# A state-space scan kernel on Trainium2: token order for `u`, exponentials written in the scan's buffer, and the state reduction moved ahead of VectorE's pieces

## The chip, the cores and the metric

One core of one Trainium2 chip. The metric is the time of one execution on the device in microseconds (us), lower is better. The program is one launch that holds four stages of a small network. The change touches only the first, the state-space stage, which runs from the start to about 4,100 us of 6,212.

## The reference, cut to what matters

The first stage is a Mamba block over x of shape (2, 4096, 512), with 1024 inner channels, 16 states per channel and a 4-tap convolution along time:

```python
hidden, gate = jnp.split(proj, 2, axis=-1)          # proj = layernorm(x) @ in_proj_w
h = causal 4-tap depthwise conv(hidden) + conv_b
hs = silu(h)
dt, Bm, Cm = split(hs @ x_proj_w)                   # each then rms-normalised
dt = softplus(dt @ dt_proj_w + dt_proj_b)
dA = exp(dt[..., None] * A)                         # (batch, time, 1024, 16)
dBu = (dt * u)[..., None] * Bm                      # u = hs
s_t = dA_t * s_{t-1} + dBu_t                        # the scan over time
y_t = sum_n s_t[n] * C_t[n]
out = ((y + u * D) * silu(gate)) @ out_proj_w
```

Everything is float32. Three more stages follow (a sum of eight matrix products, a chunked linear attention, a spline layer). They are the same in both kernels.

## The kernel before, in words

**Tiling.** Time is cut into chunks of T = 512 tokens, 8 per batch and 16 in all. One chunk is one *period*; the two batches take turns, and the middle periods are a hardware loop. The 1024 channels lie as G = 8 groups of 128 partitions. A *unit* k = 0..31 is one channel group with four of its 16 states; eight units belong to a pair of channel groups. A unit is a tile `s[k % 4]` of 128 partitions by 4 states by 512 tokens, so four units are in flight at most.

**One unit.**
- TensorE (PE) forms `BU`, the product of dt·u and B, with 16 small matmuls into four PSUM banks (`b_product`, L747). There is one `BU`, so it starts only when all scans of the unit before have read it (`scan_done`).
- ScalarE (ACT) computes the four exponentials (L507) into `DA`, two buffers of 512 tokens. Exponential n + 2 therefore waits for scan n.
- VectorE (DVE) runs the four scans (L661), `s = DA * s_before + BU`, each started from `state`.
- VectorE copies the last token of the four scans into `state` with a small reduction (L666), which raises `state_saved`. The copy is needed because the next step overwrites `s`.
- GpSimd (POOL) waits for `state_saved`, then multiplies `s` in place by the broadcast `Cb`, in two instructions of 128x1024 (L339, `z_ready`).
- TensorE adds the products of two units into `Y` by matmuls with an identity (`y_sum`, L765), in two parts, `sums(k)`, that stand behind `b_product(k)` or behind the other work of unit k. They raise `sum_done`. A slot of `s` is free when its sums are through: before, the scans waited for that.

**Work between the units.** Everything else of this period and of the next is cut into pieces and given to unit numbers by hand-written tables (`GATE_AT`, `HID_AT`, `DT_AT`, `Y_AT` and so on). Each engine walks its units in order and does its piece at its place. On VectorE `piece(k)` stands behind the scans of unit k and *ahead of* the state reduction of unit k. Its pieces are:
- k = 14..21, `conv` of one channel group: a copy of 3 elements (L543), another of 3 (L547, after a wait for ScalarE's `hid`), three `scalar_tensor_tensor` over 512 tokens (L551) with a drain between them;
- k = 0, 12, 19, 29: `dt_floor` (L581); k = 3, 13, 22, 30: `dt_max` (L586); k = 4, 13, 22, 30: `dt_times_u` (L591);
- k = 2, 10: statistics of the layer norm (L525 to L530), and k = 4, 11: its application, two `tensor_scalar` (L535);
- k = 26, 27: sums and scaling of the x projection (L557 to L573); k = 1, 9, 17, 25: `y_out` (L609), which reads PSUM; k = 3, 6, 10, 11: the residual (L599), which reads PSUM.

GpSimd has small work of its own, at k = 2 and 10 (`ln_power`, L304) and k = 26 (`ssm_power`, L308), ahead of the multiplication of that unit, and at k = 28, 29, 30 and 0 behind it (`spread_b`, L314).

On ScalarE the pieces `late(k - 1)` and `early(k)` stood between the exponentials of unit k, and `long_piece(k - 1)`, which may hold a silu over 128x2048 between two loads of the activation table, behind them.

**Two orders of the tokens.** `u` was kept block by block: token q·4 + b of a chunk at place b·128 + q. The x projection and the transposes of dt·u want blocks of 128 columns, one of each fourth token, and read them contiguously. The convolution, the product with dt and ScalarE's first write of `u` (L385) work in token order, so they step through `u` by 128 elements.

Of the kernel before, what the change touches and what calls it, by code (L numbers as in the profile page):

```python
# [58 lines left out]
def mamba_block(nc, x, in_w, chan, xproj_w, dt_w, out_w, eye, tokmask, x1):  # L59
# [21 lines left out]
    with ctx:  # L81
# [27 lines left out]
        spread = sb("spread", [P, NQ, TB, 32, 4])  # L109

        s = [sb(f"s{i}", [P, 4, T]) for i in range(SLOTS)]
        DA = [sb(f"DA{i}", [P, T]) for i in range(2)]
# [76 lines left out]
        def in_time(ap):  # L189
            return ap.rearrange("p (b q) -> p q b", b=TB)  # L190

        def by_block(ap):
            return ap.rearrange("p (q b) -> p b q", b=TB)
# [158 lines left out]
        def _(act):  # L352
# [26 lines left out]
            def take_hid(ring_, m, period, c_next, slot):  # L379

                wait(act, conv_done, c_next * G + m - 1)

                act.wait_ge(ring_.full, ring_.filled(("hid", m), period))
                bank = PJ[ring_.bank(("hid", m))]
                nc.scalar.activation(in_time(u[slot][:, m, :]), bank[:].rearrange("p (q b) -> p q b", b=TB), ACT.Identity,  # L385
                                     bias=ch[:, m, 4:5], scale=ch[:, m, 3:4])
                nc.scalar.copy(hid[m % 2][:, 3:T + 3], bank[:]).then_inc(ring_.taken["act"], 1)

            def take_gate(ring_, m, period):
# [57 lines left out]
            def body(i, b, c, first, last):  # L447
# [51 lines left out]

                for k in range(U):  # L500
                    p, nq, gi = k // UP, k % UP // 2, k % 2
                    for n in range(4):
                        if k % UP == 0 and n == 0:
                            wait(act, dt_ready, PAIRS * c + p + 1)

                        wait(act, scan_done, 4 * (c * U + k) + n - 1)
                        nc.scalar.activation(DA[n % 2][:], dt[p % 2][:, gi, :], ACT.Exp,  # L507
                                             scale=ch[:, 2 * p + gi, 7 + 4 * nq + n:8 + 4 * nq + n]).then_inc(da_ready, 1)
                        if n == 1 and k > 0:
                            late(k - 1)  # L510
                        if n == 1 and k == 0 and not first:
                            wait(act, y_ready, (c - 1) * G + 6)
                            take_gate(steady, 5, c - 1)
                        if n == 2:
                            early(k)
                    long_piece(k - 1)

            periods(act, body)

        @block.vector  # L520
        def _(dve):
# [16 lines left out]

            def conv(ring_, m, period, b_next, slot):

                out = in_time(u[slot][:, m, :])
                h_ = hid[m % 2]
                nc.vector.tensor_copy(h_[:, 0:3], hist[:, b_next, m, :])  # L543
                s_, v = ring_.emptied(("hid", m), period)
                dve.drain()
                dve.wait_ge(s_, v)
                nc.vector.tensor_copy(hist[:, b_next, m, :], h_[:, T:T + 3])  # L547
                for tap in range(3):
                    if tap > 0:
                        dve.drain()  # L550
                    last_ = nc.vector.scalar_tensor_tensor(out, h_[:, tap:tap + T].rearrange("p (q b) -> p q b", b=TB),  # L551
                                                           ch[:, m, tap:tap + 1], out, ALU.mult, ALU.add)
                last_.then_inc(conv_done, 1)

            def ssm_sums(c_next):
# [32 lines left out]
            def dt_times_u(p, n, c_of, slot):  # L588
                dve.wait_ge(u_ready, 2 * (c_of + 1))
                dve.wait_ge(dt_ready, n + 1)  # L590
                nc.vector.tensor_tensor(dts[:].rearrange("p g (b q) -> p g b q", b=TB),  # L591
                                        dt[p % 2][:].rearrange("p g (q b) -> p g b q", b=TB),
                                        u[slot][:, 2 * p:2 * p + 2, :].rearrange("p g (b q) -> p g b q", b=TB), ALU.mult
                                        ).then_inc(dtu_ready, 1)

            def add_res(ring_, j, period, c_prev):
# [27 lines left out]
            def body(i, b, c, first, last):  # L624
# [50 lines left out]
        def _(pe):  # L675
# [21 lines left out]
            def x_proj(ring_, tb, period, c_next, slot):  # L697
                use = ("xp", tb // 2)
                if tb % 2 == 0:
                    wait(pe, u_ready, 2 * (c_next + 1))  # L700
                    bank_of(ring_, use, period)
                bank = PJ[ring_.bank(use)]
                for g in range(G):
                    last_ = nc.tensor.matmul(bank[:, tb % 2 * SP_:(tb % 2 + 1) * SP_], u[slot][:, g, tb * P:(tb + 1) * P],  # L704
                                             w_xp[:, g, :], start=(g == 0), stop=(g == G - 1))
                if tb % 2 == 1:
                    last_.then_inc(ring_.full, 1)
# [20 lines left out]
            def turn_dtu(ring_, p, n, period):  # L728
                wait(pe, dtu_ready, n + 1)
                for gi in range(2):  # L730
                    bank = bank_of(ring_, (f"tr{p}", gi), period)
                    for tb in range(TB):
                        last_ = nc.tensor.transpose(bank[:, tb * P:(tb + 1) * P], dts[:, gi, tb * P:(tb + 1) * P], ident[:])
                    last_.then_inc(ring_.full, 1)

            def out_proj(bank, j, part, slot):
# [15 lines left out]
            def skip_product(p, slot):  # L752
                for r in range(2):
                    rows = slice(64 * r, 64 * r + 64)
                    for gi in range(2):
                        nc.tensor.matmul(by_block(Y[r][y_rows(r, gi), :]), skip_w[rows, 2 * p + gi, :],
                                         u[slot][rows, 2 * p + gi, :].rearrange("p (b q) -> p b q", b=TB),
                                         start=True, stop=False, tile_position=(64 * r, y_rows(r, gi).start))

            def y_sum(k_even, part):  # L760
# [1050 lines left out]
```

## Time and profile before

| what | us |
|---|---|
| median of 3 runs | 6220.06 (6214.05 to 6225.43) |
| the profiled execution | 6213.6 |
| its span from first to last instruction | 6211.7 |
| busy: PE, DVE, ACT, POOL | 5083.5, 5140.9, 2792.8, 3227.9 |
| scans (DVE, L661), 2048 of them | 2470.6 |
| z products (POOL, L339), 1024 of them | 2390.9 |

Busy is the sum of the times in which an engine has an instruction running. "L661" is line 661 of the kernel before. In a timeline a row is a run of like instructions: start, duration of the whole run, engine, line, operation, output<-inputs, count, and in brackets the idle time before it with what ended it.

### The profile page before, as it was taken

What the parts mean: (1) busy time and instruction counts of PE and PEld (TensorE: products, weight loads), DVE (VectorE), ACT (ScalarE), POOL (GpSimd) and SP (SyncE); (2) the same over time, 40 slices, a digit from 0 to 9 for tenths busy, and PEclk for the clock granted to TensorE, in tenths of its full rate; (3) what the DMA queues carried; (4) which work ended last, traced back from release to release, by engine and by line L of the source; (5) the groups of instructions that cost most, each with busy time, mean ns of one, the idle gap of its engine ahead of it and who ended that gap; (6) DMA issues with size and microseconds to landing.
All of it is one profiled execution on the core that took longest, in us unless ns stands there. A gap on an engine that the chain in (4) does not pass through costs nothing. (4 is left out here: it accounts for less than half of the span.)

```text
span 6211.7 us, 111888 instructions
## 1 busy us (share of the span) xinstructions
PE 5083.5 (82%) x41157; PEld 2990.7 (48%) x41157; DVE 5140.9 (83%) x7468; ACT 2792.8 (45%) x4180; POOL 3227.9 (52%) x1675
## 2 busy tenths in 40 slices
PE   6788988888888888888888888748888888888832
PEld 3344444444444444434434444317777776777722
DVE  4888888888888888888888888757888888888888
ACT  3656555556565555565555555512222222222200
POOL 1566665665666656657566566623333333333322
PEclk9999999999999999999999999869999999899955
DMA  2121221222212222222122221230000000000024
GB/s 81 71 96 62 89 93 65 95 73 79 89 69 89 81 77 89 76 80 89 71 89 81 77 89 72 86 130 19 23 23 21 21 23 23 19 23 23 18 96 142
DMA packets 139965, 421.36 MB, mean 68 GB/s; under 512 B 38368, under 2 KB 39904, under 8 KB 106592
## 3 DMA queue, kind: packets, MB, share of 16 engines
q1 hardware_dynamic: 136672, 411.75, 18.9%
q8 instruction: 268, 4.39, 0.3%
q10 hardware_dynamic: 2816, 3.51, 0.2%
q14 instruction: 209, 1.71, 0.1%
HBM read 361.99 MB, written 53.22 MB: 67 GB/s over the span
## 5 line engine op out<-in xcount | busy, mean ns | idle before, releaser
L339 POOL TENSOR_TENSOR s<-s,Cb 128x1024 f32<-128x1024 f32 x1024 | 2390.9, 2356 | 1362.8 <-DVE state L666 1353.3
L661 DVE TENSOR_TENSOR_SCAN s<-DA,state,BU 128x512 f32<-128x512 f32 x2048 | 2470.6, 1263 | 497.6 <-PE BU L747 301.7
L507 ACT ACTIVATE DA<-dt,ch 128x512 f32<-128x512 f32 x2048 | 1453.5, 720 | 1570.1 <-DVE s L661 1566.6
L765 PE MATMUL Y<-s,ident 64*64 64x512 f32 x8192 | 1013.0, 610 | 124.7 <-POOL s L339 124.0
L693 PE MATMUL PJ<-xnT,w_in 128*128 128x512 f32 x2048 | 998.9, 634 | 44.2 <-ACT dtuT L371 42.5
L747 PE MATMUL BU<-spread,dtuT 32*128 32x128 f32 x16384 | 624.0, 290 | 287.8 <-DVE s L661 285.5
L747 PEld LDWEIGHTS BU<-spread,dtuT 32*128 32x128 f32 x16384 | 524.0, 193 | 677.6 <-DVE s L661 544.1
L693 PEld LDWEIGHTS PJ<-xnT,w_in 128*128 128x128 f32 x2048 | 388.8, 199 | 549.0 <-issue 453.1
L765 PEld LDWEIGHTS Y<-s,ident 64*64 64x64 f32 x8192 | 280.0, 134 | 620.6 <-issue 584.9
L738 PE MATMUL PJ<-w_out,u 128*128 128x512 f32 x1024 | 481.3, 615 | 1.8 <-DVE u L609 1.5
L551 DVE SCALAR_TENSOR_TENSOR u<-hid,ch,u 128x512 f32<-128x512 f32 x384 | 434.5, 1132 | 19.1
L1121 POOL TENSOR_TENSOR x1t<-x1t,bias_b 128x512 f32<-128x512 f32 x64 | 81.0, 1266 | 525.7 <-DVE xa L1293 525.7
L1474 PE MATMUL bank<-w_high_o,aTs 128*128 128x512 f32 x512 | 212.2, 481 | 129.4 <-DVEq L1396 129.4
L738 PEld LDWEIGHTS PJ<-w_out,u 128*128 128x128 f32 x1024 | 188.7, 194 | 242.1 <-issue 231.1
L1115 POOL TENSOR_TENSOR r_t<-x,x3n 128x512 f32<-128x512 f32 x64 | 82.5, 1290 | 344.7 <-DVE x3n L1293 344.7
L1236 ACT ACTIVATE junk<-bank 128x512 f32<-128x512 f32 x64 | 38.3, 598 | 380.2 <-PE bank L1546 380.2
L1474 PEld LDWEIGHTS bank<-w_high_o,aTs 128*128 128x128 f32 x512 | 119.5, 233 | 167.3 <-issue 139.0
L1474 PE MATMUL bank<-w_high_f,xaT 128*128 128x512 f32 x512 | 195.8, 445 | 2.6 <-DVE xaT L1298 2.6
L385 ACT ACTIVATE u<-PJ,ch 128x512 f32<-128x512 f32 x128 | 162.1, 1266 | 54.7 <-PE PJ L693 52.6
L704 PE MATMUL PJ<-w_xp,u 128*128 128x160 f32 x1024 | 165.7, 322 | 22.4 <-ACT dtuT L371 12.6
L1172 ACT COPY qk_all<-bank 128x512 f32<-128x512 f32 x128 | 75.3, 588 | 224.0 <-PE bank L1474 224.0
L704 PEld LDWEIGHTS PJ<-w_xp,u 128*128 128x128 f32 x1024 | 154.4, 205 | 40.7 <-issue 26.4
(218 smaller groups left out, 7667.2 us busy)
## 6 DMA issues: line engine op xcount, KB each, us to landing
Cb<-bc SPq DMA_DIRECT2D x256, 1024.0 KB, 4.8
res<-in_x SPq DMA_DIRECT2D x64, 256.0 KB, 4.8
x<-res SPq DMA_DIRECT2D x64, 256.0 KB, 5.3
x1t<-x SPq DMA_DIRECT2D x64, 256.0 KB, 2.6
out<-r_t SPq DMA_DIRECT2D x64, 256.0 KB, 2.0
xt<-in_x SPq DMA_DIRECT2D x31, 512.0 KB, 5.3
x_all<-out SPq DMA_DIRECT2D x16, 512.0 KB, 4.1
scm<-out SPq DMA_DIRECT2D x16, 512.0 KB, 4.7
```

What stands on the lines that cost most here:

```text
L339: nc.gpsimd.tensor_tensor(pair, pair, Cb[q % 2][:, 2 * part * T:2 * part * T + 2 * T], ALU.mult).then_inc(z_ready, 1)
L385: nc.scalar.activation(in_time(u[slot][:, m, :]), bank[:].rearrange("p (q b) -> p q b", b=TB), ACT.Identity, bias=ch[:, m, 4:5], scale=ch[ ...
L507: nc.scalar.activation(DA[n % 2][:], dt[p % 2][:, gi, :], ACT.Exp, scale=ch[:, 2 * p + gi, 7 + 4 * nq + n:8 + 4 * nq + n]).then_inc(da_rea ...
L551: last_ = nc.vector.scalar_tensor_tensor(out, h_[:, tap:tap + T].rearrange("p (q b) -> p q b", b=TB), ch[:, m, tap:tap + 1], out, ALU.mult ...
L661: nc.vector.tensor_tensor_scan(s[k % SLOTS][:, n, :], DA[n % 2][:], BU[:, n::4], state[:, b, k, n:n + 1], ALU.mult, ALU.add).then_inc(scan ...
L693: last_ = nc.tensor.matmul(bank[:], w_in[:, kb, lo:lo + P], xnT[:, kb, :], start=(kb == 0), stop=(kb == KB - 1))
L704: last_ = nc.tensor.matmul(bank[:, tb % 2 * SP_:(tb % 2 + 1) * SP_], u[slot][:, g, tb * P:(tb + 1) * P], w_xp[:, g, :], start=(g == 0), st ...
L738: last_ = nc.tensor.matmul(bank[:], u[slot][:, g, j * P:(j + 1) * P], w_out[:, g, :], start=(g == 0), stop=(g == G - 1))
L747: last_ = nc.tensor.matmul(BU[:, i * T:(i + 1) * T].rearrange("p (t b n) -> p b t n", b=TB, n=4)[:, tb], dtuT[rows, gi, tb, :], spread[row ...
L765: last_ = nc.tensor.matmul(Y[r][y_rows(r, gi), :], ident[rows, rows], s[(k_even + gi) % SLOTS][rows, n, :], start=False, stop=(n == 3 and ...
L1115: nc.gpsimd.tensor_tensor(r_t[s_][:], x3[s_][:], x3n[s_][:], ALU.add).then_inc(S["r_ready"], 1)
L1474: last_ = nc.tensor.matmul(b_[:], src[part][:, k, :], wt, start=(k == 0 and i == 0), stop=(k == KB - 1 and i == 2))
```

## The change

Four edits, all in the state-space stage.

1. `u` is in token order everywhere. ScalarE, the convolution and the product with dt step by 1; the x projection's weights and the transposes' inputs are now read with a step of 4 elements (`by_block`), and the skip product reads and writes straight.
2. ScalarE writes the exponentials into the scan's own buffer `s[k % 4]`; the scan works in place and `DA` is gone. The wait for a free slot (`sum_done`) moves from VectorE's scans to ScalarE's exponentials, and their wait for `scan_done` is gone.
3. ScalarE computes the four exponentials of unit k in one go. `long_piece(k - 1)`, `late(k - 1)` and `early(k)` follow, in this order.
4. On VectorE the state reduction comes straight behind the scans of its unit, and `piece(k)` behind the reduction.

```diff
@@ ScalarE, take_hid
-                nc.scalar.activation(in_time(u[slot][:, m, :]), bank[:].rearrange("p (q b) -> p q b", b=TB), ACT.Identity,
-                                     bias=ch[:, m, 4:5], scale=ch[:, m, 3:4])
+                nc.scalar.activation(u[slot][:, m, :], bank[:], ACT.Identity, bias=ch[:, m, 4:5], scale=ch[:, m, 3:4])
...
@@ ScalarE, body
                 for k in range(U):
                     p, nq, gi = k // UP, k % UP // 2, k % 2
+                    if k % UP == 0:
+                        wait(act, dt_ready, PAIRS * c + p + 1)
+                    wait(act, sum_done, c * U + k // 2 * 2 - 2)
                     for n in range(4):
-                        if k % UP == 0 and n == 0:
-                            wait(act, dt_ready, PAIRS * c + p + 1)
-
-                        wait(act, scan_done, 4 * (c * U + k) + n - 1)
-                        nc.scalar.activation(DA[n % 2][:], dt[p % 2][:, gi, :], ACT.Exp,
+                        nc.scalar.activation(s[k % SLOTS][:, n, :], dt[p % 2][:, gi, :], ACT.Exp,
                                              scale=ch[:, 2 * p + gi, 7 + 4 * nq + n:8 + 4 * nq + n]).then_inc(da_ready, 1)
-                        if n == 1 and k > 0:
-                            late(k - 1)
...
-                        if n == 2:
-                            early(k)
                     long_piece(k - 1)
+                    if k > 0:
+                        late(k - 1)
...
+                    early(k)
@@ VectorE, conv
-                out = in_time(u[slot][:, m, :])
+                out = u[slot][:, m, :]
...
-                    last_ = nc.vector.scalar_tensor_tensor(out, h_[:, tap:tap + T].rearrange("p (q b) -> p q b", b=TB),
-                                                           ch[:, m, tap:tap + 1], out, ALU.mult, ALU.add)
+                    last_ = nc.vector.scalar_tensor_tensor(out, h_[:, tap:tap + T], ch[:, m, tap:tap + 1], out,
+                                                           ALU.mult, ALU.add)
@@ VectorE, dt_times_u
-                nc.vector.tensor_tensor(dts[:].rearrange("p g (b q) -> p g b q", b=TB),
-                                        dt[p % 2][:].rearrange("p g (q b) -> p g b q", b=TB),
-                                        u[slot][:, 2 * p:2 * p + 2, :].rearrange("p g (b q) -> p g b q", b=TB), ALU.mult
+                nc.vector.tensor_tensor(dts[:], dt[p % 2][:], u[slot][:, 2 * p:2 * p + 2, :], ALU.mult
@@ VectorE, body
                 for k in range(U):
-                    wait(dve, sum_done, c * U + k // 2 * 2 - 2)
                     wait(dve, dbu_ready, c * U + k + 1)
                     for n in range(4):
                         wait(dve, da_ready, 4 * (c * U + k) + n + 1)
-                        nc.vector.tensor_tensor_scan(s[k % SLOTS][:, n, :], DA[n % 2][:], BU[:, n::4],
+                        nc.vector.tensor_tensor_scan(s[k % SLOTS][:, n, :], s[k % SLOTS][:, n, :], BU[:, n::4],
                                                      state[:, b, k, n:n + 1], ALU.mult, ALU.add
                                                      ).then_inc(scan_done, 1)
-                    piece(k)
                     wait(dve, scan_done, 4 * (c * U + k + 1))
                     nc.vector.tensor_reduce(state[:, b, k, :], s[k % SLOTS][:, :, T - 1:T], AX.X, ALU.max
                                             ).then_inc(state_saved, 1)
+                    piece(k)
@@ TensorE: x_proj reads by_block(u[slot][:, g, :])[:, tb], turn_dtu by_block(dts[:, gi, :])[:, tb],
@@ skip_product writes Y and reads u straight.
```

**VectorE, a unit with a convolution.** Before, from the scans of the first such unit on:

```order
L661 SCALAR_TENSOR_TENSOR s<-DA,state,BU 128x512 [waits da_ready,dbu_ready,sum_done]
L661 SCALAR_TENSOR_TENSOR s<-DA,state,BU 128x512 [waits da_ready] x3
L543 COPY hid<-hist 128x3
L547 COPY hist<-hid 128x3 [waits proj_taken_act_steady]
L551 SCALAR_TENSOR_TENSOR u<-hid,ch,u 128x128x4 x3
L666 TENSOR_REDUCE state<-s 128x4 [waits scan_done]
```

And now, at the same place:

```order
L651 SCALAR_TENSOR_TENSOR s<-s,state,BU 128x512 [waits da_ready,dbu_ready]
L651 SCALAR_TENSOR_TENSOR s<-s,state,BU 128x512 [waits da_ready] x3
L655 TENSOR_REDUCE state<-s 128x4 [waits scan_done]
L536 COPY hid0<-hist 128x3
L540 COPY hist<-hid0 128x3 [waits proj_taken_act_steady]
L544 SCALAR_TENSOR_TENSOR u1<-hid0,ch,u1 128x512 x3
```

The rows with SCALAR_TENSOR_TENSOR on `s` are the scans. The reduction that frees GpSimd moved from behind the three passes over `u` to directly behind the scans, and the wait for `sum_done` is gone from the first scan.

**ScalarE, around the first silu of the gate (k = 5 and 6).** Before:

```order
L507 ACTIVATE DA0<-dt0,ch 128x512 [waits scan_done]
L507 ACTIVATE DA1<-dt0,ch 128x512 [waits scan_done]
L491 ACT_TABLE_LOAD
L491 ACTIVATE gate<-gate 128x2048
L492 ACT_TABLE_LOAD
L507 ACTIVATE DA0<-dt0,ch 128x512 [waits scan_done]
```

And now:

```order
L501 ACTIVATE s2<-dt0,ch 128x512 [waits sum_done]
L501 ACTIVATE s2<-dt0,ch 128x512 x3
L486 ACT_TABLE_LOAD
L486 ACTIVATE gate<-gate 128x2048
L487 ACT_TABLE_LOAD
L501 ACTIVATE s3<-dt0,ch 128x512 [waits sum_done]
L501 ACTIVATE s3<-dt0,ch 128x512 x3
```

Each exponential waited for a scan; now a unit's four wait once, for the sums that free their slot.

## Rows read from the trace of the kernel before

**Rows 1.** Stretch, us; busy us (count) PE, PEld, DVE, ACT, POOL; PE clock; DMA

```profile
400.00:3700.00 3300.00, 2892.06 (x25117) 1379.67 (x25109) 2841.09 (x3241) 1950.24 (x2632) 2079.57 (x941) 0.98 0.23 82
```

**Rows 2.** Who waited for whom, 400 to 3700 us: total us, times, longest

```profile
DVE s L661 <- PE BU L747: 240.6, 181, 3.8
DVE s L661 <- ACT DA L507: 134.7, 124, 3.3
```

**Rows 3.** Timeline of DVE: unit 14 of the ninth period, and unit 22's start

```profile
2216.57 4.78 DVE L661 TENSOR_TENSOR_SCAN s<-DA,state,BU 128x512 f32<-128x512 f32 x4
2221.27 0.15 DVE L543 COPY hid<-hist 128x3 f32<-128x3 f32 x1
2221.57 0.17 DVE L547 COPY hist<-hid 128x3 f32<-128x3 f32 x1 [0.15 <-issue]
2221.65 3.63 DVE L551 SCALAR_TENSOR_TENSOR u<-hid,ch,u 128x512 f32<-128x512 f32 x3
2225.20 0.15 DVE L666 TENSOR_REDUCE state<-s 128x4 f32<-128x4 f32 x1
...
2288.57 4.78 DVE L661 TENSOR_TENSOR_SCAN s<-DA,state,BU 128x512 f32<-128x512 f32 x4
```

**Rows 4.** Timeline of POOL, the product of the same unit 14

```profile
2225.43 4.67 POOL L339 TENSOR_TENSOR s<-s,Cb 128x1024 f32<-128x1024 f32 x2 [4.03 <-DVE state L666]
```

**Rows 5.** Timelines of POOL and DVE near 889 us

```profile
885.82 4.67 POOL L339 TENSOR_TENSOR s<-s,Cb 128x1024 f32<-128x1024 f32 x2 [1.99 <-DMA Cb<-bc]
889.60 1.97 DVE L586 TENSOR_TENSOR dt<-dt,dts 128x1024 f32<-128x1024 f32 x1 [0.24 <-DVE res L599]
```

**Rows 6.** Timelines of DVE and POOL near 5894 us, in a later stage

```profile
5893.54 0.69 DVE L1408 TENSOR_TENSOR rc<-qk_all,rot 128x512 f32<-128x512 f32 x1
5893.70 1.68 POOL L1126 TENSOR_TENSOR xf<-xf,gamma_b 128x512 f32<-128x512 f32 x1 [7.31 <-DVE xf L1293]
5894.14 1.52 DVE L1410 TENSOR_TENSOR rs<-qk_all,rot 128x256 f32<-128x256 f32 x1
```

**Rows 7.** Timelines of POOL and DVE near 4228 us, in a later stage

```profile
4227.67 1.05 POOL L1138 TENSOR_TENSOR kd<-qk_all,k_dec 128x512 f32<-128x512 f32 x1
4227.97 1.03 DVE L1293 TENSOR_SCALAR xb<-x_all,mv_b,rd_b 128x512 f32<-128x512 f32 x1
4228.68 1.46 POOL L1147 TENSOR_TENSOR kvd<-kv,kv_dec 128x512 f32<-128x512 f32 x1
```

**Rows 8.** Groups by line and shape, 1000 to 3800 us: busy us, mean ns, idle before

```profile
L551 DVE SCALAR_TENSOR_TENSOR u<-hid,ch,u 128x512 f32<-128x512 f32 x278 | 314.8, 1132 | 13.9
L704 PEld LDWEIGHTS PJ<-w_xp,u 128*128 128x128 f32 x729 | 111.1, 207 | 23.1 <-ACT dtuT L371 11.5 <-issue 10.1
L591 DVE TENSOR_TENSOR dts<-dt,u 128x1024 f32<-128x1024 f32 x45 | 92.1, 2046 | 3.5
L586 DVE TENSOR_TENSOR dt<-dt,dts 128x1024 f32<-128x1024 f32 x45 | 55.1, 1223 | 13.9 <-ACT dts L423 11.4 <-DVE res L599 2.5
```

**Rows 9.** Timeline of DVE, scan starts of units 3, 4, 5, 11, 12, 13, 27, 28

```profile
2134.18 4.79 DVE L661 TENSOR_TENSOR_SCAN s<-DA,state,BU 128x512 f32<-128x512 f32 x4 [0.82 <-PE BU L747]
...
2141.00 4.78 DVE L661 TENSOR_TENSOR_SCAN s<-DA,state,BU 128x512 f32<-128x512 f32 x4
...
2148.62 4.78 DVE L661 TENSOR_TENSOR_SCAN s<-DA,state,BU 128x512 f32<-128x512 f32 x4
...
2194.43 4.79 DVE L661 TENSOR_TENSOR_SCAN s<-DA,state,BU 128x512 f32<-128x512 f32 x4
...
2201.16 3.62 DVE L661 TENSOR_TENSOR_SCAN s<-DA,state,BU 128x512 f32<-128x512 f32 x3
...
2207.90 4.79 DVE L661 TENSOR_TENSOR_SCAN s<-DA,state,BU 128x512 f32<-128x512 f32 x4 [0.98 <-PE BU L747]
...
2324.55 4.79 DVE L661 TENSOR_TENSOR_SCAN s<-DA,state,BU 128x512 f32<-128x512 f32 x4 [1.22 <-PE BU L747]
...
2331.16 3.62 DVE L661 TENSOR_TENSOR_SCAN s<-DA,state,BU 128x512 f32<-128x512 f32 x3 [0.30 <-PE BU L747]
```

More of the change, by code:

```diff
@@ L111, in mamba_block @@
         s = [sb(f"s{i}", [P, 4, T]) for i in range(SLOTS)]
-        DA = [sb(f"DA{i}", [P, T]) for i in range(2)]
         Cb = [sb(f"Cb{i}", [P, 4 * T]) for i in range(2)]
@@ L187, in y_rows @@
             return slice(at, at + 64)
-        def in_time(ap):
-            return ap.rearrange("p (b q) -> p q b", b=TB)
         def by_block(ap):
@@ L501, in body @@
                     p, nq, gi = k // UP, k % UP // 2, k % 2
+                    if k % UP == 0:
+                        wait(act, dt_ready, PAIRS * c + p + 1)
+                    wait(act, sum_done, c * U + k // 2 * 2 - 2)
                     for n in range(4):
-                        if k % UP == 0 and n == 0:
-                            wait(act, dt_ready, PAIRS * c + p + 1)
-                        wait(act, scan_done, 4 * (c * U + k) + n - 1)
-                        nc.scalar.activation(DA[n % 2][:], dt[p % 2][:, gi, :], ACT.Exp,
+                        nc.scalar.activation(s[k % SLOTS][:, n, :], dt[p % 2][:, gi, :], ACT.Exp,
                                              scale=ch[:, 2 * p + gi, 7 + 4 * nq + n:8 + 4 * nq + n]).then_inc(da_ready, 1)
-                        if n == 1 and k > 0:
-                            late(k - 1)
-                        if n == 1 and k == 0 and not first:
-                            wait(act, y_ready, (c - 1) * G + 6)
-                            take_gate(steady, 5, c - 1)
-                        if n == 2:
-                            early(k)
-                    long_piece(k - 1)
+                    long_piece(k - 1)
+                    if k > 0:
+                        late(k - 1)
+                    elif not first:
+                        wait(act, y_ready, (c - 1) * G + 6)
+                        take_gate(steady, 5, c - 1)
+                    early(k)
             periods(act, body)
@@ L703, in x_proj @@
                 for g in range(G):
-                    last_ = nc.tensor.matmul(bank[:, tb % 2 * SP_:(tb % 2 + 1) * SP_], u[slot][:, g, tb * P:(tb + 1) * P],
+                    last_ = nc.tensor.matmul(bank[:, tb % 2 * SP_:(tb % 2 + 1) * SP_], by_block(u[slot][:, g, :])[:, tb],
                                              w_xp[:, g, :], start=(g == 0), stop=(g == G - 1))
@@ L732, in turn_dtu @@
                     for tb in range(TB):
-                        last_ = nc.tensor.transpose(bank[:, tb * P:(tb + 1) * P], dts[:, gi, tb * P:(tb + 1) * P], ident[:])
+                        last_ = nc.tensor.transpose(bank[:, tb * P:(tb + 1) * P], by_block(dts[:, gi, :])[:, tb], ident[:])
                     last_.then_inc(ring_.full, 1)
@@ L755, in skip_product @@
                     for gi in range(2):
-                        nc.tensor.matmul(by_block(Y[r][y_rows(r, gi), :]), skip_w[rows, 2 * p + gi, :],
-                                         u[slot][rows, 2 * p + gi, :].rearrange("p (b q) -> p b q", b=TB),
+                        nc.tensor.matmul(Y[r][y_rows(r, gi), :], skip_w[rows, 2 * p + gi, :], u[slot][rows, 2 * p + gi, :],
                                          start=True, stop=False, tile_position=(64 * r, y_rows(r, gi).start))
```

## The prediction

> **What bounds the kernel now.** I read the busy time by stretch first. From 400 to 3700 us, inside the state-space stage, VectorE is busy 2841 of 3300 us and TensorE 2892, the matmul figure being a modelled one, at a granted clock of 0.98 of full speed [rows 1]. No engine is free to spare, so order matters. Then the waits: VectorE waits 240.6 us there for `BU` and 134.7 us for exponentials [rows 2]. A period lasts about 249 us (45 products with dt in 2800 us, four per period [rows 8]), so the stretch holds 13.2 periods, and these waits are 18.2 and 10.2 us of each. The `BU` wait is structural: one `BU`, made only after the unit's last scan. The change leaves it. The wait for exponentials is what edits 2 and 3 can remove.
>
> The third view is the timeline of one unit with a convolution, 14 [rows 3, 4]. Scans start at 2216.57; the first copy starts at 2221.27, so 4.70 us later VectorE turns to its piece; three passes over `u` take 3.63; only then comes the reduction, at 2225.20, and the product on GpSimd starts 0.23 later and runs 4.67 for its two halves. It fits under the next unit's 4.78 of scans. So in the kernel before, VectorE's pieces run while GpSimd stands still, and GpSimd runs beside scans. Eight such units take 2288.57 − 2216.57 = 72.0 us [rows 3].
>
> **Two engines that exclude each other.** Three places tell what happens when a piece does meet GpSimd. At 889.60 `dt_max`, two inputs in SBUF, starts while the product runs until 885.82 + 4.67 = 890.49. It ends at 891.57, 1.08 later [rows 5]; its mean is 1.223 [rows 8]. It did nothing until GpSimd was through, then needed its own time less 0.14. At 5894.14 a product of 256 elements starts beside a GpSimd instruction that ends at 5895.38 and is itself done at 5895.66: 1.52 us, of which 1.24 are waiting [rows 6]. There GpSimd had asked at 5893.70, under the VectorE instruction L1408 that ended at 5894.23; VectorE's next instruction was ready at once, and GpSimd still came first. At 4228 it is the reverse: GpSimd's L1138 ends at 4228.72, its next one, L1147, is already there at 4228.68, and VectorE's, waiting since 4227.97, ends first, at 4229.00 [rows 7]. So whoever waits gets the next turn, and they alternate by whole instructions. The Trainium skill ("SBUF — State Buffer", Who interferes with whom) says that a VectorE instruction with two SBUF inputs or in a two-port mode, and a GpSimd one, block each other fully, the first to start going first. It gives no order among those who wait; by its words alone both this forecast and rival A stand, and rows 6 and 7 choose between them.
>
> Scans read one input from SBUF and one from PSUM, and rows 3 and 4 have them beside the product at full speed. `y_out` and the residual read PSUM too, and count as free.
>
> **The change part by part** (times from the start of the reduction in its new place, 4.70 us after the unit's first scan).
>
> *Convolution units, 14 to 21.* The first copy starts at 0.08 and ends at 0.23. GpSimd starts at 0.23 [rows 4]. The second copy would start at 0.38 (0.30 after the first [rows 3]): I take it that it waits, until 0.23 + 2.34 = 2.57. GpSimd's second half is queued by then and goes next, to 4.95. First pass: in token order it costs 0.69, the price of a contiguous two-input operation of 512 elements (L1408 [rows 6]), less 0.14, so it ends at 5.50. Two passes more, 0.69 + 0.05 each: 6.98. The next scan starts 0.08 before the end of what stands ahead of it (the reduction starts 0.08 before the passes' end [rows 3]). Unit: 4.70 + 6.98 − 0.08 = 11.6 us. Eight of them and 0.6 for `dt_floor` in unit 19: 93.4, against 72.0: **+21.4 us**. Without the lock the passes would have saved 3 x (1.13 − 0.69) = 1.3 per unit.
>
> *Other units with pieces that need both ports* [rows 9]:
> - Unit 3: residual, then `dt_max`, behind one half of the product: 2.57 + 1.09 = 3.66; unit 8.3 against 6.82: +1.5.
> - Unit 4: `ln_apply` gets in first (0.08 to 0.61), a half to 2.95, second `ln_apply` 3.23, the other half 5.57, `dt_times_u` 1.09 more, 6.66. Unit 11.3 against 7.62: +3.7. The product with dt itself falls from 2046 to about 1223 ns [rows 8].
> - Unit 11: `ln_apply` twice around one half, 3.23, residual 0.67: 8.5 against 6.73: +1.8.
> - Unit 13: `dt_max` first, to 1.30, a half to 3.64, `dt_times_u` to 4.73: 9.35 against 8.67: +0.7. Units 22 and 30 hold the same two pieces: +0.8 each.
> - Unit 27: three scalings. The product of unit 26 is still running (it stands behind `ssm_power`) until about 0.9; the first scaling ends at 1.4, then half, scaling, half, scaling: 6.2. Unit 10.8 against 6.61: +4.2.
> - `dt_floor` at 0, 12 and 29 starts 0.15 before GpSimd can: nothing for VectorE.
>
> Together 13.5. **Lost per period: 34.9 us.**
>
> *Exponentials.* A unit's four no longer wait for scans. The gate is `sum_done`: unit k even needs the sums of the pair before last, which TensorE issues right behind the `BU` of unit k − 1, about a unit ahead. The silu over 2048 columns with its two table loads then falls on exponentials that are already there. Of the 10.2 us, 1 lies in the convolution units and is in their 72.0; some waits end in the `BU` wait instead. I take **7.8 us gained per period**, bounds 0 and 10.2. Late is then only `BU`. Nothing queues behind ScalarE's one new wait, since it can be a unit ahead.
>
> *ScalarE's write of `u`* gets cheaper and is hidden on an engine busy 59% [rows 1]: nothing. *Earlier products* cannot help where VectorE sets the pace: nothing. No DMA changes; `Cb` loads are released by the products and have a unit to spare.
>
> *TensorE's reads with a step of 4.* 32 weight loads of 207 ns per period [rows 8] and 32 transposes. No row of before shows such a read. Bounds: nothing, or as much as the step of 128 costs VectorE, a factor of 2046/1223 = 1.7: 32 x 0.14 = 4.5 us for the loads, and about the same for the transposes. I take nothing, since nearly all units then go at VectorE's pace, with TensorE waiting for scans; the upper end would be +9 x 15 = 135 us if none were hidden. The Trainium skill ("SBUF — State Buffer", SBUF: two separate sides) has lines of 16 bytes and a penalty for each access that crosses to a new one; a step of 4 floats does so every time, and by that the sum would move towards this upper end.
>
> *Prologue.* 8 groups of 3 passes, 0.44 less each [rows 6, 8], 10.6 in all, a part of it under the projections: −8.
>
> **Sum.** Net per period 34.9 − 7.8 = +27.1. Fifteen periods prepare a next chunk: +406. The last has units 3, 4, 13 and 22 without norm and convolution: about −5. With the prologue: 6213.6 + 406 − 5 − 8 = 6606.6 for the profiled execution, which lies 6.5 under the median of the runs; I predict **6610 us**, some 6% slower.
>
> **Own range of this case.** The passes may stay at 1.13 (+1.3 per unit, +160), TensorE's reads +135, exponentials 0 to 10.2 gained (+117 or −36), a second copy that does not wait (first pass ahead of the second half, −0.3 per unit, −36), two scalings going together in unit 27 and at `ln_apply` (−2.3 each, −70). Not all come at once: 6450 to 6780.
>
> **Rivals.**
> - **A, faster: VectorE keeps its turn.** If GpSimd cannot get in between two instructions of one piece, a convolution unit pays one half only: 2.6 + 3 x 0.74 − 0.14 gives 9.3, +0.4 each over 72.0/8 = 9.0, +3 in all; unit 3 +1.5; units 4, 11, 13, 22, 27 and 30 about −3 together. With −7.8: −6.3 per period, −95, less 8: 6115 by the median. Decides: whether the passes run in a row after the first half. For it: the pauses between them are only 0.05. Against: rows 6. 7%.
> - **B, faster: no conflict to speak of.** Passes of 0.74 beside GpSimd: convolution units about 7.8 by TensorE's own work, −10; the other pieces −3; −7.8. Times 15: about −310, 5900. Rows 5 to 7 speak against it. 5%.
> - **C, much slower: the turns cost more than their halves**, or the exponentials, tied to sums that wait for slower products, become late. Each 1 us more in eight units is +120: 6800 to 7000. 5%.
> - **D, the pieces have moved where GpSimd is mostly waiting anyway**, for `Cb` or an earlier product, and both effects about cancel: 6200 to 6450. A wait of 1.99 for `Cb` is there [rows 5], but the one of unit 14 is for the reduction [rows 4]. 6%.
>
> **How the numbers follow.** The forecast has 77%. Range for 8 in 10: its own, widened a little at the lower end for D: 6420 to 6790. A measurement of this kernel tells 0.2% from no change. Faster: A, B and little of D, 0.13. Same: 0.02. Slower: 0.85.
>
> **What would show it.** In the changed profile the passes over `u` must have a mean near (5.50 − 0.46 + 2 x 0.74)/3, some 2.2 us, though they are cheaper; the product on GpSimd must start 0.2 behind each unit's scans; its waits for `state` must be gone from the top, and VectorE's waits for exponentials be near nothing; units 14 to 21 must take 11 to 12 us each and unit 5, with no piece, as long as before. Passes of 0.7 us beside a running product would prove the lock wrong, and a mean of 1.3 with 9.3 us units rival A.

## The result and the profile after

The changed kernel takes 6723.91 us (median of 4 runs, 6717.08 to 6729.63) against 6222.25 before, a ratio of 1.081, 95% interval 1.079 to 1.083. It is slower, as forecast, and 114 us above the predicted 6610. Its profiled execution has a span of 6715.3 us.

The groups of instructions by line and shape, 1000 to 3800 us of the changed kernel (busy us, mean ns of one | idle before), answer to [rows 8]:

```profile
L544 DVE SCALAR_TENSOR_TENSOR u<-hid,ch,u 128x512 f32<-128x512 f32 x240 | 331.7, 1382 | 11.9
L540 DVE COPY hist<-hid 128x3 f32<-128x3 f32 x80 | 175.9, 2199 | 13.8 <-issue 10.1
L584 DVE TENSOR_TENSOR dts<-dt,u 128x1024 f32<-128x1024 f32 x40 | 129.5, 3238 | 3.1
L579 DVE TENSOR_TENSOR dt<-dt,dts 128x1024 f32<-128x1024 f32 x39 | 58.2, 1493 | 2.1 <-DVE res L590 2.1
L528 DVE TENSOR_SCALAR xt<-xt,mv,rstd 128x512 f32<-128x512 f32 x38 | 57.7, 1560 | 0.0
L566 DVE TENSOR_TENSOR xt<-xt 128x64 f32<-128x64 f32 x20 | 46.6, 2366 | 0.0
L694 PEld LDWEIGHTS PJ<-w_xp,u 128*128 128x128 f32 x640 | 151.6, 329 | 13.2 <-issue 8.1 <-ACT dtuT L367 3.8
```

A pass over `u` steps by 1 now and is yet longer, 1382 ns against 1132. The product with dt, whose access became contiguous too, went from 2046 to 3238. The clearest row is L540: a copy of three elements takes 2.2 us on average. None of these computes longer: with GpSimd out of the way (first experiment below) the same four groups take 749, 169, 1223 and 530 ns (L544, L540, L584, L528). They stand on VectorE, issued, and wait for GpSimd. The last row is TensorE's and another matter: the weight loads with a step of 4 cost 329 ns, not 207.

One unit shows how. The timeline of VectorE in the changed kernel, unit 15 of a period (as [rows 3]):

```profile
2504.48 4.79 DVE L651 TENSOR_TENSOR_SCAN s<-s,state,BU 128x512 f32<-128x512 f32 x4
2509.30 0.16 DVE L655 TENSOR_REDUCE state<-s 128x4 f32<-128x4 f32 x1
2509.37 0.16 DVE L536 COPY hid<-hist 128x3 f32<-128x3 f32 x1
2509.68 2.23 DVE L540 COPY hist<-hid 128x3 f32<-128x3 f32 x1 [0.15 <-issue]
2511.82 4.56 DVE L544 SCALAR_TENSOR_TENSOR u<-hid,ch,u 128x512 f32<-128x512 f32 x3
2516.30 4.79 DVE L651 TENSOR_TENSOR_SCAN s<-s,state,BU 128x512 f32<-128x512 f32 x4
```

and that of GpSimd beside it (as [rows 4]):

```profile
2509.53 4.66 POOL L335 TENSOR_TENSOR s<-s,Cb 128x1024 f32<-128x1024 f32 x2 [7.17 <-DVE state L655]
```

The product starts 0.23 after the reduction. The second copy, issued at 2509.68, ends at 2511.91, when the first half is through; the second half goes next, to 2514.19, and the passes only end at 2516.38. The unit takes 11.82 us against the 9.0 of before.

Who waited for whom, 400 to 3700 us of the changed kernel, answers to [rows 2]:

```profile
DVE s L651 <- PE BU L737: 264.2, 180, 5.7
DVE s L651 <- ACT s L501: 16.2, 7, 3.2
```

The waits for exponentials are down from 134.7 us to 16.2: edits 2 and 3 do what they say. GpSimd's own waits for `state`, the same view before and after, did not shrink:

```profile
POOL s L339 <- DVE state L666: 1101.0, 385, 5.6
POOL s L335 <- DVE state L655: 1231.4, 295, 7.8
```

Scan starts in the changed kernel, from the timeline of VectorE (as [rows 9]; units 3, 4, 5, 11, 12, 13, 14, 22, 23, 24, 25, 27, 28 of one period):

```profile
2689.63 4.79 DVE L651 TENSOR_TENSOR_SCAN s<-s,state,BU 128x512 f32<-128x512 f32 x4 [0.68 <-PE BU L737]
...
2698.56 4.78 DVE L651 TENSOR_TENSOR_SCAN s<-s,state,BU 128x512 f32<-128x512 f32 x4
...
2709.70 4.78 DVE L651 TENSOR_TENSOR_SCAN s<-s,state,BU 128x512 f32<-128x512 f32 x4
...
2753.33 4.80 DVE L651 TENSOR_TENSOR_SCAN s<-s,state,BU 128x512 f32<-128x512 f32 x4 [0.32 <-DVE res L590]
...
2762.20 4.79 DVE L651 TENSOR_TENSOR_SCAN s<-s,state,BU 128x512 f32<-128x512 f32 x4 [0.32 <-DVE res L590]
...
2768.37 4.79 DVE L651 TENSOR_TENSOR_SCAN s<-s,state,BU 128x512 f32<-128x512 f32 x4 [0.55 <-PE BU L737]
...
2777.75 4.78 DVE L651 TENSOR_TENSOR_SCAN s<-s,state,BU 128x512 f32<-128x512 f32 x4
...
2873.16 4.79 DVE L651 TENSOR_TENSOR_SCAN s<-s,state,BU 128x512 f32<-128x512 f32 x4
...
2882.53 4.78 DVE L651 TENSOR_TENSOR_SCAN s<-s,state,BU 128x512 f32<-128x512 f32 x4
...
2889.44 4.79 DVE L651 TENSOR_TENSOR_SCAN s<-s,state,BU 128x512 f32<-128x512 f32 x4 [1.94 <-PE BU L737]
...
2900.11 4.79 DVE L651 TENSOR_TENSOR_SCAN s<-s,state,BU 128x512 f32<-128x512 f32 x4 [5.69 <-PE BU L737]
...
2914.52 4.79 DVE L651 TENSOR_TENSOR_SCAN s<-s,state,BU 128x512 f32<-128x512 f32 x4 [1.33 <-PE BU L737]
...
2925.24 4.78 DVE L651 TENSOR_TENSOR_SCAN s<-s,state,BU 128x512 f32<-128x512 f32 x4
```

The eight convolution units take 2873.16 − 2777.75 = 95.4 us. Unit 24 takes 2900.11 − 2889.44 = 10.67, of which VectorE waits 5.69 for `BU`.

### The profile page after: what moved, and what is told of

Same layout as the page of the kernel before. It is cut to its first block and busy times, and to the rows that moved or that the text cites. A ratio compares the mean times of both kernels' runs of the same rounds, so it can differ in the third digit from the quotient of the medians.

```text
span 6715.3 us, 110904 instructions
## 1 busy us (share of the span) xinstructions
PE 5323.7 (79%) x41157; PEld 3151.7 (47%) x41157; DVE 5720.9 (85%) x7468; ACT 2611.6 (39%) x4180; POOL 3377.3 (50%) x1675
## 5 line engine op out<-in xcount | busy, mean ns | idle before, releaser
L335 POOL TENSOR_TENSOR s<-s,Cb 128x1024 f32<-128x1024 f32 x1024 | 2539.7, 2502 | 1678.4 <-DVE state L655 1670.1
L651 DVE TENSOR_TENSOR_SCAN s<-s,state,BU 128x512 f32<-128x512 f32 x2048 | 2452.7, 1259 | 426.3 <-PE BU L737 382.4
L501 ACT ACTIVATE s<-dt,ch 128x512 f32<-128x512 f32 x2048 | 1305.3, 712 | 921.6 <-PE Y L754 920.4
L754 PE MATMUL Y<-s,ident 64*64 64x512 f32 x8192 | 1088.6, 650 | 17.9 <-POOL s L335 17.6
L544 DVE SCALAR_TENSOR_TENSOR u<-hid,ch,u 128x512 f32<-128x512 f32 x384 | 532.3, 1386 | 19.1
L540 DVE COPY hist<-hid 128x3 f32<-128x3 f32 x128 | 248.5, 1942 | 34.2 <-ACT hid L382 15.8
L694 PE MATMUL PJ<-w_xp,u 128*128 128x160 f32 x1024 | 252.9, 404 | 9.6 <-issue 6.5
L694 PEld LDWEIGHTS PJ<-w_xp,u 128*128 128x128 f32 x1024 | 243.0, 329 | 27.2 <-issue 20.8
L367 ACT COPY dtuT<-PJ 128x512 f32<-128x512 f32 x128 | 68.8, 588 | 394.0 <-PE PJ L723 394.0
L584 DVE TENSOR_TENSOR dts<-dt,u 128x1024 f32<-128x1024 f32 x64 | 203.1, 3174 | 5.0
```

The source lines that it names most:

```text
L335: nc.gpsimd.tensor_tensor(pair, pair, Cb[q % 2][:, 2 * part * T:2 * part * T + 2 * T], ALU.mult).then_inc(z_ready, 1)
L501: nc.scalar.activation(s[k % SLOTS][:, n, :], dt[p % 2][:, gi, :], ACT.Exp, scale=ch[:, 2 * p + gi, 7 + 4 * nq + n:8 + 4 * nq + n]).then_i ...
L584: nc.vector.tensor_tensor(dts[:], dt[p % 2][:], u[slot][:, 2 * p:2 * p + 2, :], ALU.mult).then_inc(dtu_ready, 1)
L651: nc.vector.tensor_tensor_scan(s[k % SLOTS][:, n, :], s[k % SLOTS][:, n, :], BU[:, n::4], state[:, b, k, n:n + 1], ALU.mult, ALU.add).then ...
L754: last_ = nc.tensor.matmul(Y[r][y_rows(r, gi), :], ident[rows, rows], s[(k_even + gi) % SLOTS][rows, n, :], start=False, stop=(n == 3 and ...
```

## The experiments

Each ratio is to the kernel before on the same chip. A unit's length is the time from its first scan to the next unit's, averaged over 12 middle periods of the trace.

**Undoing edit 4 alone.**

```diff
+                    piece(k)
                     wait(dve, scan_done, 4 * (c * U + k + 1))
                     nc.vector.tensor_reduce(state[:, b, k, :], s[k % SLOTS][:, :, T - 1:T], AX.X, ALU.max
                                             ).then_inc(state_saved, 1)
-                    piece(k)
```

> The changed kernel with edit 4 alone undone: piece(k) stands ahead of the state reduction again. Theory (VectorE's two-port pieces and GpSimd's product exclude each other): convolution units fall from 11.8 us to about 8.0, where TensorE's own work of 7 to 9 us sets them, units 3, 4, 11, 13, 22, 27 and 30 lose another 13 us, so some 44 us per period go: about 6070 us, 2 to 3% below the kernel before. Rival (scans in place, the new gate on the exponentials or TensorE's reads with a step of 4 are what costs): still above 6500 us.

Measured: 5924.77 us, ratio 0.954 (0.952 to 0.956). The rival is out: edits 1 to 3 together are good for 4.6%, and edit 4 turns that into a loss of 8%. It came 145 us lower than I expected: the convolution units are 7.5 us in most, 62 for the eight, and the units behind a long one are shorter too (more below). Its passes are free of waiting:

```profile
L544 DVE SCALAR_TENSOR_TENSOR u<-hid,ch,u 128x512 f32<-128x512 f32 x264 | 197.7, 749 | 13.1
```

This row of its groups by line and shape, 1000 to 3800 us, gives the own price of a pass, 749 ns. The 1382 of the changed kernel is this and 0.63 us of waiting.

**Edit 4 alone on the kernel before.**

```diff
-                    piece(k)
                     wait(dve, scan_done, 4 * (c * U + k + 1))
                     nc.vector.tensor_reduce(...).then_inc(state_saved, 1)
+                    piece(k)
```

> The kernel before with edit 4 alone. Theory: the passes over u still cost 1.13 us each, so a convolution unit is 4.70 + 4.95 + 0.99 + 2 x 1.18 - 0.08 = 12.9 us against 9.0, +32 per period; the other units with two-port pieces +15; about 45 us x 15, so 6900 us. Rival (edit 4 is harmless and edits 1 to 3 made the kernel slower): 6220 us.

Measured: 7034.94 us, ratio 1.133 (1.131 to 1.135). One moved instruction of 0.15 us costs 13%. The period went from 249.5 to 304.0 us, 54.5 more where the terms I had named are 32 and 15. The convolution units, 13.1 each, are the 32. The other units whose pieces meet GpSimd (3, 4, 11, 13, 22, 27, 30) are 20.9, not 15; units 13 and 30 alone add 3.8 and 3.7, since `dt_max` waits there as well (2531 ns on average, 1493 in the changed kernel). Units without a lock add a little, as 31 (9.8 against 7.9) and 5 (7.3 against 6.4). Its row for the passes, same view and stretch:

```profile
L551 DVE SCALAR_TENSOR_TENSOR u<-hid,ch,u 128x512 f32<-128x512 f32 x216 | 377.8, 1749 | 10.7
```

1749 is the 1132 of before and 0.62 us of waiting, the same surcharge as with the contiguous pass.

**The reduction early, GpSimd's start late.**

```diff
-                    nc.vector.tensor_reduce(state[:, b, k, :], s[k % SLOTS][:, :, T - 1:T], AX.X, ALU.max
-                                            ).then_inc(state_saved, 1)
+                    nc.vector.tensor_reduce(state[:, b, k, :], s[k % SLOTS][:, :, T - 1:T], AX.X, ALU.max)
                     piece(k)
+                    dve.drain().then_inc(state_saved, 1)
```

> The changed kernel; the reduction stays directly behind the scans, but the signal that lets GpSimd start is given by a drain behind piece(k). Theory (it is GpSimd's start that costs, not the place of the reduction): as e1_piece_first within 0.5%, about 6080 us. Rival (the reduction between scans and piece costs by itself, or the order of VectorE's instructions does): near 6720 us.

Measured: 5985.2 us, ratio 0.964 (0.962 to 0.965). VectorE's instructions have the order of the changed kernel, and the loss is gone: it is when GpSimd starts. It is 1.0% above the kernel with the piece first, twice what I had allowed. A convolution unit is 0.5 us longer. Some 0.2 of this is the reduction in its new place: the piece starts 4.91 us after the unit's first scan, not 4.70, so a small part of the rival is true. The other 0.3 is a wait of the next scan for nothing the profile names (44.8 us in 3300), which the kernel with the piece first has not; the drain is the only thing added there. The row is from who waited for whom, 400 to 3700 us, of this kernel (total us, times, longest):

```profile
DVE s L651 <- issue: 44.8, 156, 0.6
```

Per period it is 6.0 us above the kernel with the piece first (236.8 against 230.8), some 90 us over fifteen. The total differs by only 60, because everything behind the last scan, the same code in both, took 2105 us here and 2128 there. No run tells why.

**GpSimd's product in quarters.**

```diff
-                    for part in range(2):
-                        pair = s[k % SLOTS][:, 2 * part:2 * part + 2, :].rearrange("p n t -> p (n t)")
-                        nc.gpsimd.tensor_tensor(pair, pair, Cb[q % 2][:, 2 * part * T:2 * part * T + 2 * T],
-                                                ALU.mult).then_inc(z_ready, 1)
+                    for n in range(4):
+                        last_ = nc.gpsimd.tensor_tensor(s[k % SLOTS][:, n, :], s[k % SLOTS][:, n, :],
+                                                        Cb[q % 2][:, n * T:(n + 1) * T], ALU.mult)
+                        if n % 2 == 1:
+                            last_.then_inc(z_ready, 1)
```

> The changed kernel with GpSimd's product in four instructions of 512 elements, not two of 1024 (signals as before, at the second and the fourth). Theory (turns alternate by whole instructions): VectorE waits for one quarter, about 1.2 us, where it waited for a half, 2.3: units 4 and 27 lose 2.3 us each, 3, 11, 13, 22 and 30 1.15 each, the convolution units 0.4 each, some 13 us per period, about 6530 us. Rival (VectorE waits until the whole product is through): no change, 6720 us, or a little slower by GpSimd's fixed cost per instruction.

Measured: 6516.83 us, ratio 1.049 (1.047 to 1.051). The period fell from 284.1 to 271.1 us, by about the 13 I had named; unit 4 from 11.15 to 8.97, unit 27 from 10.72 to 8.85, unit 13 from 9.38 to 8.29, most convolution units from 11.84 to 11.38. A convolution unit in this kernel's timelines of VectorE and of GpSimd:

```profile
2401.33 1.15 DVE L541 COPY hist<-hid 128x3 f32<-128x3 f32 x1 [0.15 <-issue]
2402.39 5.17 DVE L545 SCALAR_TENSOR_TENSOR u<-hid,ch,u 128x512 f32<-128x512 f32 x3
...
2401.18 5.83 POOL L334 TENSOR_TENSOR s<-s,Cb 128x512 f32<-128x512 f32 x4 [5.53 <-DVE state L656]
```

The copy now waits 1.15 where it waited 2.23, and GpSimd's four quarters spread to 5.83 because VectorE's turns lie between them. Turns by whole instructions are shown; "VectorE waits until the product is through" is out.

**Edits 2 and 3 alone, and edit 1 alone,** both on the order of before (piece, then reduction). The first is the changed ScalarE body and the in-place scans on a block-ordered `u`; the second is all of the diff that concerns `u`, with `DA` kept.

```diff
@@ e5, against the kernel before
-                        nc.vector.tensor_tensor_scan(s[k % SLOTS][:, n, :], DA[n % 2][:], BU[:, n::4],
+                        nc.vector.tensor_tensor_scan(s[k % SLOTS][:, n, :], s[k % SLOTS][:, n, :], BU[:, n::4],
... and ScalarE's body as in the whole diff
@@ e6, against the kernel before
-                out = in_time(u[slot][:, m, :])
+                out = u[slot][:, m, :]
... and all other lines of the whole diff that read or write u
```

> The kernel before with edits 2 and 3 alone (exponentials in the scan's buffer, a unit's four in one go); u in block order, the piece ahead of the reduction. Theory: the waits for exponentials go (10.2 us per period in the profile before, 7.8 of them worth something, mostly units 6 and 9): 6210 - 7.5 x 15, about 6100 us. Rival (the waits turn into waits for BU and nothing is won): 6200 us.

Measured: 6023.04 us, ratio 0.970 (0.968 to 0.971), 77 below my figure. The period is 237.5 us, 12.0 less, more than the 10.2 of VectorE's own waits for exponentials: units 6 and 9 give 2.1 and 1.9, units 28 and 29 1.2 and 1.3, and unit 23, where before TensorE waited for ScalarE's copies, 1.0. From 1000 to 3800 us TensorE's waits for these copies fall from 8.9 us to under 1 ahead of the transposes of dt·u and from 9.8 to 2.9 ahead of the x projection. That ScalarE serves TensorE earlier because it is no longer tied to scans is my reading of this, not a separate test.

> The kernel before with edit 1 alone (u in token order). Theory: passes of 0.75 us take 1.2 us from each convolution unit, as far as TensorE's own work lets it (-9 per period), the product with dt -2, TensorE's reads with a step of 4 +4 (units 24 and 25, as in the changed kernel's trace): -7 x 15, about 6100 us. Rival (convolution units stay as they are, bound by TensorE or ScalarE): 6260 us.

Measured: 6146.31 us, ratio 0.989 (0.988 to 0.991). A gain of 1.0%, where I expected 1.8%. The convolution units gave the 9 us per period I had named (8.7), but units 24 and 25 are 3.1 and 0.8 us longer, as in the changed kernel, and unit 23 another 1.0.

**TensorE's reads contiguous.**

```diff
@@ x_proj, against e1_piece_first
-                    last_ = nc.tensor.matmul(bank[...], by_block(u[slot][:, g, :])[:, tb],
+                    last_ = nc.tensor.matmul(bank[...], u[slot][:, g, tb * P:(tb + 1) * P],
@@ turn_dtu
-                        last_ = nc.tensor.transpose(bank[...], by_block(dts[:, gi, :])[:, tb], ident[:])
+                        last_ = nc.tensor.transpose(bank[...], dts[:, gi, tb * P:(tb + 1) * P], ident[:])
```

The expectation names only the x projection. As built, the kernel reads the transposes' inputs contiguously too. The transposes stand in units 7, 15, 23 and 31; units 24 and 25 hold none, so what they show is the x projection's alone.

> e1_piece_first with one more change: the x projection reads its weights contiguously out of u (128 neighbouring places instead of each fourth), so it projects other tokens than the reference does. Theory (the step of 4 lengthens the weight loads from 205 to 329 ns and makes unit 24 3.2 us longer, unit 25 0.8): about 4 us per period less, 5865 us, and unit 24 back at 7.5 us. Rival (unit 24 is long for another reason, such as the order of TensorE's work or its clock): 5925 us.

Measured: 5837.4 us, ratio 0.940 (0.938 to 0.941), 87 us under the kernel with the step of 4 (that one ran on another chip; the kernel before takes 6209 us there and 6212 here). Unit 24 is back at 7.53, unit 25 at 6.18, unit 23 at 6.17. The groups of this kernel, 1000 to 3800 us:

```profile
L694 PE MATMUL PJ<-w_xp,u 128*128 128x160 f32 x704 | 104.4, 304 | 2.7 <-ACT dtuT L367 2.7
L694 PEld LDWEIGHTS PJ<-w_xp,u 128*128 128x128 f32 x704 | 96.5, 190 | 15.5 <-issue 9.5 <-ACT dtuT L367 4.8
```

and the same two with the step of 4, in the kernel with the piece first:

```profile
L694 PE MATMUL PJ<-w_xp,u 128*128 128x160 f32 x707 | 174.8, 403 | 2.2 <-ACT dtuT L367 2.2
L694 PEld LDWEIGHTS PJ<-w_xp,u 128*128 128x128 f32 x706 | 167.3, 328 | 14.5 <-issue 9.4 <-ACT dtuT L367 3.8
```

The step alone is worth 99 ns per matmul and 138 per load. The period falls from 230.8 to 225.4 us: 3.15 in unit 24, 1.1 in unit 23 and 0.8 in unit 25 are nearly all of it.

**GpSimd's product short.**

```diff
-                        pair = s[k % SLOTS][:, 2 * part:2 * part + 2, :].rearrange("p n t -> p (n t)")
-                        nc.gpsimd.tensor_tensor(pair, pair, Cb[q % 2][:, 2 * part * T:2 * part * T + 2 * T],
+                        pair = s[k % SLOTS][:, 2 * part:2 * part + 1, 0:8].rearrange("p n t -> p (n t)")
+                        nc.gpsimd.tensor_tensor(pair, pair, Cb[q % 2][:, 2 * part * T:2 * part * T + 8],
```

> The changed kernel, but GpSimd multiplies 8 elements per instruction instead of 1024 (most of the product with C is left out). Theory (what costs in the changed kernel is the time for which GpSimd holds the port): convolution units fall to what TensorE allows, near 7.5 us, and the time to that of e1_piece_first, 5925 us, or a little under. Rival (each turn costs something fixed, whatever its length): convolution units stay over 9 us and the time over 6200 us.

Measured: 5939.03 us, ratio 0.956 (0.955 to 0.958). Most convolution units take 7.6 us, passes 749 ns. With the order of the changed kernel and all its signals, a short turn costs next to nothing: the price is the length of GpSimd's instructions.

**The place chosen by unit.**

```diff
+                    early_state = k not in (3, 4, 11, 13, 22, 27, 30) and not 14 <= k <= 21
+                    if not early_state:
+                        piece(k)
                     wait(dve, scan_done, 4 * (c * U + k + 1))
                     nc.vector.tensor_reduce(...).then_inc(state_saved, 1)
-                    piece(k)
+                    if early_state:
+                        piece(k)
```

> The changed kernel with the place of the reduction chosen by unit: behind the piece in units 3, 4, 11, 13 to 22, 27 and 30, whose pieces need both ports, directly behind the scans in all others. Theory: no piece meets GpSimd in a way that costs, and GpSimd starts 1 to 2 us earlier in units with y_out, statistics or a residual, where VectorE did not wait for it anyway: as e1_piece_first, 5925 us, within 0.5%. Rival (the earlier start is worth something to TensorE's sums, which e1_piece_first's trace has waiting for GpSimd in units 18 and 28): 1% or more under it, 5865 us. Rival (one of the other pieces meets GpSimd after all): over 6000 us.

Measured: 5922.44 us, ratio 0.953 (0.952 to 0.954), the same as with the piece first everywhere. The earlier start harms nowhere in these units and is worth nothing: VectorE's next scan never waited for it. Both are faster than the kernel before and the changed one.

## Why the prediction was right

Point by point, by its own units, in averages over 12 periods.

| step | predicted, us per period | measured |
|---|---|---|
| convolution units 14 to 21 | +21.4 | +23.1 |
| unit 3, 4, 11 | +1.5, +3.7, +1.8 | +1.4, +3.5, +2.1 |
| unit 13, 22, 30 | +0.7, +0.8, +0.8 | +0.7, +0.9, +0.7 |
| unit 27 | +4.2 | +4.1 |
| exponentials (0, 6, 7, 8, 9, 12, 28, 29, 31) | −7.8 | −7.0 |
| TensorE's reads (23, 24, 25) | 0 | +4.1 |
| unit 5 | 0 | +0.8 |
| net | +27.1 | +34.7 |

**The mechanism** was the right one. VectorE's pieces of the kinds listed there and GpSimd's product exclude each other, and they take turns by instruction. Rivals A and B fell in the trace (no convolution unit takes 9.3 us or 7.8) and with the quarters. C asked for over 6800 us; D for a GpSimd that is waiting anyway. Scans stay out of it: they take 1259 ns each in the changed kernel, 1263 before, where they run beside the product, and 1260 with the short product of 0.3 us. Undoing edit 4 shows that edits 1 to 3 help by themselves, and giving only GpSimd's signal late shows what in edit 4 costs.

**Two of my own signs failed**, and neither speaks against the mechanism. I asked for passes with a mean near 2.2 us; it is 1.38. The 2.2 lets the first pass start at 0.46, though by my own timeline the second copy holds VectorE until 2.57; with that, (5.50 − 2.57 + 2 x 0.74)/3 = 1.47. In the unit shown, the copy waits for one half (2.23 us) and the first pass for the other (2.91 us; the two behind it 0.75 each). So 1.38 looks like rival A's 1.3, but A has one wait in a unit and 9.3 us, and here are two and 11.8. I also asked that GpSimd's waits for `state` be gone from the top. They are still first and grew from 1101.0 to 1231.4 us: GpSimd starts earlier, and then stands longer until the scans of a longer unit are through.

**The convolution units** were 1.7 us per period too cheap. I priced a pass at 0.69 us by another operation, and this one takes 0.75 alone, with 0.07 between passes, not 0.05. And I let the reduction start 4.70 us after the unit's first scan, where a piece would. It starts at 4.82, since it waits for the last scan's signal. The kernel before shows this in its unit 5, which has no piece; its scans start at 2148.62 [rows 9]:

```profile
2153.44 0.16 DVE L666 TENSOR_REDUCE state<-s 128x4 f32<-128x4 f32 x1
```

**The exponentials** gave 7.0 of my 7.8 us in their units. On the order of before, edits 2 and 3 gave 12.0 in all, above my upper bound of 10.2, which counted only VectorE's own waits.

**The term that was mis-sized** is TensorE's reads, "I take nothing". The bounds I gave held the answer; the choice in them was wrong. I also counted 32 loads, as the source has them, where the row itself says 64 per period (729 in 2800 us); each of these matmuls appears twice in the trace. And my reason, that VectorE sets the pace nearly everywhere, did not hold for unit 24: two tiles of the x projection stand there with sums and no long piece on VectorE, so all of it shows, as 5.69 us of waiting for `BU`, where the kernel before has 2.54. These two tiles in TensorE's timelines, before and in the changed kernel:

```profile
2303.15 4.61 PE L704 MATMUL PJ<-w_xp,u 128*128 128x160 f32 x32
2889.21 7.76 PE L694 MATMUL PJ<-w_xp,u 128*128 128x160 f32 x32
```

They are 3.15 us longer, and so is unit 24. The contiguous read takes it back to 7.53. The 4.1 us of the table are over half of the missing 7.6 per period, and the reads cost more than that: 5.0 by the contiguous run, since edits 2 and 3 take 1.0 off unit 23 by themselves.

**Unit 5** has no piece and got longer, 7.19 against 6.36. TensorE in the changed kernel, behind the long unit 4, from its timeline:

```profile
2703.40 1.17 PE L737 MATMUL BU<-spread,dtuT 32*128 32x128 f32 x32 [1.80 <-DVE s L651]
...
2714.54 2.09 PE L737 MATMUL BU<-spread,dtuT 32*128 32x128 f32 x32 [4.46 <-DVE s L651]
```

and the busy time by stretch, units 4 and 5 and then that second product alone (us; busy PE, PEld, DVE, ACT, POOL; clock; DMA):

```profile
2698.50:2709.70 11.20, 9.39 (x75) 3.64 (x73) 11.17 (x9) 3.75 (x6) 7.44 (x3) 1.00 0.38 119
2709.70:2717.10 7.40, 2.94 (x34) 2.30 (x34) 4.95 (x6) 6.43 (x7) 2.34 (x2) 0.80 0.00 0
2714.50:2716.65 2.15, 2.11 (x33) 1.89 (x33) 0.16 (x1) 1.67 (x3) 1.89 (x1) 0.50 0.00 0
```

After 4.46 us without work the same matmuls (16 in the source, 32 in the rows) take 2.09 us, not 1.17. The last line is that product alone: its granted clock is 0.50 of full speed, so it ran at 1.2 GHz, not 2.4. Over the same 12 periods the product behind unit 5's scans takes 2.02 us on average, each time after 4.46 or 4.47 us of idleness. In the kernel before it is 1.17 after 0.7 to 0.95 us, and in the kernel with the piece first 1.17 in all 12. The difference, 0.85, is the 0.82 that unit 5 got longer. A VectorE that is stuck lets TensorE stand, and the next `BU`, which is on the path, is made slowly. Over 400 to 3700 us the granted clock is 0.93, where [rows 1] has 0.98. I had no term for this. No run changed the clock by itself.

**The sum.** 7.6 us more in each of 15 periods is 114, the distance between 6610 and 6724, but that it meets so exactly is luck. All fifteen periods together took 512 us more than before, where I had 406; the ones at the ends grew less than the middle ones. The prologue, which I put at −8, gave 0.3: the first scan starts at 121.5 us, before at 121.9. It starts at 117.7 with the contiguous reads and at 122.1 without them (piece first in both), so the slower reads cost some 4 us there as well. With the last period and what follows it (−8.5), the span grew by 503.6 us, against 393 in my sum.

## What to carry to other kernels

Before an instruction is moved, ask what it *releases*: the reduction itself costs 0.15 us wherever it stands, but it starts GpSimd, and started in the middle of VectorE's pieces it cost 13% on both kernels (6209 to 7035 us, 5925 to 6724). GpSimd's product is best put beside VectorE instructions that did not wait for it in these traces: scans, `y_out` (686 ns, 675 before) and the residual (688, 678 before), which read one input from PSUM; where that can't be, shorter GpSimd instructions make shorter turns (6724 us with halves, 6517 with quarters). And a layout change has to be priced at every reader: the order that shortens VectorE's passes from 1132 to 749 ns makes each weight load of the x projection 138 ns longer.

## What the runs showed of the hardware that I had not expected

- A copy of three elements waits for a whole GpSimd instruction like any other: 2.23 us behind a half, 1.15 behind a quarter, 0.17 alone. Its size says little about its price when GpSimd is at work.
- Weight loads from SBUF with a step of 4 floats take 328 ns where contiguous ones take 190, and the matmuls 403 where 304. The Trainium skill ("SBUF — State Buffer", SBUF: two separate sides) has a penalty for every access that crosses to a new line of 16 bytes; these rows agree with it in kind, and give the size.
- Behind 4.46 us in which TensorE stood idle, the granted clock was 0.50 of full speed, and the next `BU` product took 2.09 us in place of 1.17. So an engine that waits for another can slow a third that is not part of the conflict.
